# Setup order and the lead of the row maxima at the start of a two-layer AdaLN transformer kernel

## What is computed

```
mod = (silu(L0_c) @ L0_wmod).reshape(8, 6, 1, 128)
sa, ca, ga, sb, cb, gb = mod[:, 0], ..., mod[:, 5]
h = layernorm(x) * (1 + ca) + sa
q, k, v = h @ Wq + bq, h @ Wk + bk, h @ Wv + bv          # per head
scores = where(causal, -1e9, q @ k.T / sqrt(8))
x = x + ga * ((softmax(scores) @ v) @ Wo + bo)
```

## Time and profile before

| | |
|---|---|
| median of 3 runs | 1028.89 us (1027.29 to 1029.31) |
| the profiled execution | 1028.94 us, its span 1027.2 us |
| PE busy | 931.0 us (91%) |
| DVE busy | 776.5 us (76%) |
| ACT busy | 747.8 us (73%) |
| POOL busy | 541.3 us (53%) |
| chain that ended last | reaches back only into the last stage |

### The profile page before, as it was taken

One profiled execution on the slowest core, in us unless ns is written; L12 is line 12 of the kernel. 1 busy time (PEld: TensorE's weight loads), 2 busy tenths in 40 slices (PEclk: granted clock), 3 DMA queues, 4 the chain that ended last, 5 costly groups with the idle time before them and its releaser, 6 DMA issues. The chain is left out here.

```text
span 1027.2 us, 23002 instructions
## 1 busy us (share of the span) xinstructions
PE 931.0 (91%) x8664; PEld 513.0 (50%) x8664; DVE 776.5 (76%) x1319; ACT 747.8 (73%) x1380; POOL 541.3 (53%) x755
## 2 busy tenths in 40 slices
PE   4789989889888999999999799999999999989896
PEld 3234343343436888888888533333333333333575
DVE  4778878878864776767777678979788898994476
ACT  2388878878786566666665488888888888889663
POOL 4376766677632121322111078687777869666343
PEclk8599999999999999999999999999999999999999
DMA  7323332221104522425233021211202021100011
GB/s 181 96 74 121 114 104 78 74 76 50 51 26 124 167 82 74 114 90 148 61 106 96 20 84 30 59 35 53 75 14 77 13 84 35 56 13 14 25 32 52
DMA packets 63598, 73.91 MB, mean 72 GB/s; under 512 B 14136, under 2 KB 46008, under 8 KB 63104
## 3 DMA queue, kind: packets, MB, share of 16 engines
q1 hardware_dynamic: 62336, 69.23, 23.5%
q10 hardware_dynamic: 1152, 3.21, 1.0%
HBM read 39.24 MB, written 2.77 MB: 41 GB/s over the span
## 5 line engine op out<-in xcount | busy, mean ns | idle before, releaser
L872 ACT ACTIVATE at_E<-at_Sb 128x512 f32<-128x512 f32 x832 | 440.9, 597 | 75.7 <-PE at_Sb L718 70.2
L944 DVE TENSOR_REDUCE mx<-at_Mb 128x2 f32<-128x1024 f32 x242 | 280.6, 1216 | 40.3 <-PE at_Mb L681 39.1
L718 PE MATMUL at_Sb<-QP,KP 64*128 64x512 bf16 (+3 forms) x1024 | 202.3, 342 | 16.7 <-ACT full_k L419 7.1
L766 PE MATMUL at_Ob<-at_E,VP 128*32 128x256 f32 (+2 forms) x2816 | 204.5, 371 | 2.2 <-POOL at_E L1046 1.0
L1046 POOL TENSOR_TENSOR at_E<-at_E,factor 128x512 f32<-128x512 f32 x128 | 162.3, 1273 | 65.3 <-ACT at_E L872 55.7
L681 PE MATMUL at_Mb<-KP,QP 62*128 62x512 bf16 x996 | 169.7, 348 | 8.5 <-DVE mx L944 6.5
L947 DVE TENSOR_REDUCE mx<-at_Mb 128x2 f32<-128x768 f32 (+1 forms) x128 | 136.7, 1085 | 52.9 <-PE at_Mb L681 51.8
L1057 POOL TENSOR_SCALAR_AFFINE_SELECT at_E<-at_E 128x512 f32<-128x512 f32 x128 | 80.0, 645 | 71.8 <-ACT at_E L872 71.8
L718 PEld LDWEIGHTS at_Sb<-QP,KP 64*128 64x128 bf16 x1024 | 73.5, 95 | 82.6 <-ACT at_E L872 37.9
L766 PEld LDWEIGHTS at_Ob<-at_E,VP 128*32 128x32 f32 x2816 | 58.2, 108 | 88.1 <-issue 65.6
L1498 DVE TENSOR_TENSOR ex_hh<-ex_R,ex_th 128x512 f32<-128x512 f32 x88 | 64.6, 734 | 49.4 <-ACT ex_th L1435 48.7
(11 more groups left out here) (213 smaller groups left out, 1441.8 us busy)
## 6 DMA issues: line engine op xcount, KB each, us to landing
QP<-q SPq DMA_DIRECT2D x96, 128.0 KB, 2.4
KP<-k SPq DMA_DIRECT2D x91, 128.0 KB, 2.4
ex_R<-rw_dram SPq DMA_DIRECT2D x32, 256.0 KB, 3.5
ctxN<-Oev SPq DMA_DIRECT2D x16, 256.0 KB, 2.5
denB<-rdram SPq DMA_DIRECT2D x64, 64.0 KB
ex_R<-rw_dram SPq DMA_DIRECT2D x16, 224.0 KB, 3.5
ex_R<-rw_dram SPq DMA_DIRECT2D x16, 192.0 KB, 3.3
ex_R<-rw_dram SPq DMA_DIRECT2D x16, 160.0 KB, 2.8
```

The costliest lines, as they stand in the source:

```text
L718: return pe.matmul(out[:, at:at + SEQ - q0], KP[p0:p0 + ROWS_H, b % 2, 2 * g + a, kt * P:(kt + 1) * P], QP[p0:p0 + ROWS_H, b % 2, 2 * g + ...
L766: last = pe.matmul(Ob[VW * i:VW * (i + 1), 0, q0:q1], weights_of(b, G, kt, i, q0), moving, start=(kt == 0 and q0 == 0), stop=False, skip_g ...
L872: nc.scalar.activation(dst, src, ACT.Exp).then_inc(s["s_read"], 1)
L944: v.tensor_reduce(mx[:, G % 2, :, t % 2, t // 2], src, AX.X, ALU.max).then_inc(s["m_read"], 1)
```

## The change

In the setup: x of batch 0 is loaded ahead of c; POOL's zero fill of VP moves ahead of `front_powers`; batch 0's `front_normalise` moves from POOL to DVE; on PE the transposes of `xn` move ahead of bv times Wo.

In layer 0's attention: nine beats of maxima instead of eleven stand ahead of beat 0 (ten maxima ahead of the first score), and beats 2 and 5 hold two maxima each, the second at the end of PE's beat, so that the lead is eleven again from there. `max_T(1)` moves from beat 2 to beat 4, `max_T(0)` to beat -2. `shifts(G)` follows the table `shifts_at` (one beat after the last maximum of the group): beat -3 for group 0, 3 for group 1, as before from group 2 on. Statistics and `xn` of batch 1 move to beats -2 and -1.

```diff
         @block.sync
-            sp.dma_start(cT[:], dram["c"]).then_inc(s["c"], 16)
             sp.dma_start(x[:, 0:SEQ].rearrange("p (t d) -> p t d", t=TILES),
                          dram["x"][0].rearrange("(t p) d -> p t d", p=P)).then_inc(s["x0"], 16)
+            sp.dma_start(cT[:], dram["c"]).then_inc(s["c"], 16)
...
             g.memset(sb["ones"][:], 1.0)
+            g.memset(sb["VP"][:], 0.0).then_inc(s["zero"], 1)
             front_powers(g, sb, front, 0)
-            front_normalise(g, sb, front, 0)
-            g.memset(sb["VP"][:], 0.0).then_inc(s["zero"], 1)
...
+            t.wait_ge(s["ident"], 1)
+            front_transpose(t, sb, front, 0, fb[:, 0, :])
             t.wait_ge(s["columns"], 16)
...
-            t.wait_ge(s["ident"], 1)
-            front_transpose(t, sb, front, 0, fb[:, 0, :])
...
             front_aggregate(v, sb, front, 0)
+            front_normalise(v, sb, front, 0)
...
-        LEAD = 11 if causal else LEAD1
-        START = -LEAD if causal else 0
+        START = -9 if causal else 0
+        DOUBLE_AT = (2, 5) if causal else ()
...
+        first_max = 2 if causal else 0
...
-            if (beat + 4) % BPG == 0 and 0 <= (beat + 4) // BPG < ALLG:
+            if (beat + 4) % BPG == 0 and first_max <= (beat + 4) // BPG < ALLG:
                 out.append(("max", (beat + 4) // BPG))
+            if causal and beat in (-2, 4):
+                out.append(("max", 0 if beat < 0 else 1))
...
-        def m_of(beat):
-
-            m = beat + LEAD
-            return divmod(m, BPG) if 0 <= m < BPG * ALLG else None
+        def ms_of(beat):
+
+            m = beat + (9 if causal else LEAD1) + sum(at < beat for at in DOUBLE_AT)
+            return [divmod(i, BPG) for i in range(m, m + 1 + (beat in DOUBLE_AT)) if 0 <= i < BPG * ALLG]
...
+            for m in ms_of(beat):
+                m_slot[("max",) + m] = len(m_slot)
+                if m[1] == BPG - 1:
+                    shifts_at[beat + 1] = m[0]
...
-                if m_of(beat) is not None:
-                    max_score(*m_of(beat))
+                for m in ms_of(beat)[0:1]:
+                    max_score(*m)
...
+                for m in ms_of(beat)[1:]:
+                    max_score(*m)
...
-                if causal and beat == -4:
+                if causal and beat == -2:
                     v.wait_ge(sb["x1"], 16)
...
-                G, off = divmod(beat + LEAD - BPG, BPG)
-                if off == 0 and 0 <= G < ALLG:
-                    shifts(G)
-                if causal and beat == -3:
+                if beat in shifts_at:
+                    shifts(shifts_at[beat])
+                if causal and beat == -1:
                     front_powers(p, sb, s, 1)
                     normalise(1)
```

More of the change, by code:

```diff
@@ L607, in out_of @@
             return n - 1 if at == OUT_AT and 1 <= n <= last_b else None
-        def m_of(beat):
-            m = beat + LEAD
-            return divmod(m, BPG) if 0 <= m < BPG * ALLG else None
-        s_slot, m_slot = {}, {}
+        def ms_of(beat):
+            m = beat + (9 if causal else LEAD1) + sum(at < beat for at in DOUBLE_AT)
+            return [divmod(i, BPG) for i in range(m, m + 1 + (beat in DOUBLE_AT)) if 0 <= i < BPG * ALLG]
+        s_slot, m_slot, shifts_at = {}, {}, {}
         for name in (("ln", 0), ("q", 0), ("k", 0), ("v", 0)):
@@ L618, in attention_phase @@
             s_slot[("max", 0)] = len(s_slot)
-            for m in range(LEAD):
+            for m in range(LEAD1):
                 m_slot[("max",) + divmod(m, BPG)] = m
@@ L623, in attention_phase @@
                 s_slot[name] = len(s_slot)
-            if m_of(beat) is not None:
-                m_slot[("max",) + m_of(beat)] = len(m_slot)
+            for m in ms_of(beat):
+                m_slot[("max",) + m] = len(m_slot)
+                if m[1] == BPG - 1:
+                    shifts_at[beat + 1] = m[0]
             if out_of(beat) is not None:
@@ L962, in _ @@
             for beat in range(START, END):
-                if m_of(beat) is not None:
-                    reduce_max(*m_of(beat))
+                for m in ms_of(beat):
+                    reduce_max(*m)
                 if out_of(beat) is not None:
```

## The result

The changed kernel took 1035.11 us in the median of its first 4 runs (1032.15 to 1036.4), against 1028.09 for the kernel before beside it (4 runs): ratio 1.0065, 95% interval 1.0038 to 1.0092. Ten more runs of the same kernel gave a median of 1033.34 against 1029.53 (33 runs), ratio 1.0043 (1.0021 to 1.0066), that is +4.4 us (+2.2 to +6.8). It is slower. The forecast of +3.5 us (a ratio of 1.0034) lies in the second interval, and just under the lower end of the first; the first median, 1035.11, is only 0.09 us inside the upper end of the forecast range (1035.2). The profiled execution took 1032.15 us, with a span of 1030.4 against 1027.2.

A forecast was written before the change was run, and what follows sets the result against it. The prediction saw PE busy 91% of the span, and waits setting the first group's pace. Setup -0.7, stall +2.6 and clock +1.6 gave +3.5 us on 1028.94: 1032.4 us, range 1029.7 to 1035.2.

The forecast's parts named there:

- buy two exps, no more: First group: the first scores run some 2.5 us earlier, but batch 1's transposes still wait for xn, so only two exps are gained.
- The stall's size: Beat 4: PE waits for group 1's shifts behind q's split, +3.4 us, less 0.8 won back: +2.6, bounds 1.9 to 3.4.
- the setup's -0.7: Setup: projections start at about 11.4 in place of 12.14, -0.7 us, bounds 0 to -1.0.
- the stall without the clock: Rival: PE's clock rises as early as before and stays, leaving setup and stall: +1.9 us, 1030.9 us; chance 0.18.
- The clock's size: First group: PE's clock rises later or falls again around beats 5 and 6: +1.6 us, between 0 and 2.6.
- Every later group by the same amount: After the first group: the first Oev is 2 to 5 us later, and each later group is equally late.
- the stall is taken up: Rival: PE waits in beat 4, but slack in later groups wins nearly all back: 1028.2 to 1029.5 us; chance 0.09.
- no stall: Rival: POOL finishes split and shifts before PE reaches the transpose in beat 4: -0.7 to -2.3, about 1026.8 us; chance 0.05.
- The clock costs more: Rival: the clock falls in the stall and again, or more stretches run at half clock: +5 to +7, about 1034.8 us; chance 0.10.
- the main case: Stall in beat 4 and slower clock behind it together: 1031.6 to 1034.2 us, chance 0.58.
- nothing: Setup: loading x ahead of c delays c by at most one queue place, at no cost to PE.
- the consequence I drew from it: Setup: the moved fill holds the second silu step until 5.2, so xn ends at about 9.4 and the sum is 0.2 us higher.

The follow-up runs named there:

- shift_first: The changed kernel with group 1's shifts one beat earlier on POOL, ahead of the split of batch 1's q: 1028.71 us, ratio 0.9996 to the kernel before.
- fill_stall: The changed kernel with ten matmuls of unread result on PE directly ahead of its wait for group 1's shifts: 1030.79 us, ratio 1.0011 to the kernel before.
- after_again: The whole changed kernel measured once more, with no edit: median 1033.34 us in ten runs, ratio 1.0043 to the kernel before.
- stats_old_lead: The changed kernel's setup with the old lead of eleven maxima and batch 1's statistics, rstd and xn ahead of the first loop: 1027.43 us, ratio 0.9991.
- fill_late: The changed kernel with POOL's zero fill of VP behind front_powers again, beside xn on DVE: 1035.2 us, ratio 1.0068 to the kernel before.
- late_shift: The kernel before with only group 1's shifts put behind q's split on POOL and their transpose moved to beat 4: 1032.14 us, ratio 1.0039.

## Why the prediction was right, and where it was off

**Direction and mechanism: right.** Every sign that the prediction named for the stall is there: first scores at 34.18 (forecast 34.8), then a wait of 2.77 us (over 2), `nm` and `nmx` right behind the split, 2.97 us of waiting at L667 (2 or more), a clock back at 0.50, the first `Oev` 2.4 us later (2 to 5). That the earlier first scores "buy two exps, no more" agrees with the runs: q's projection starts 1.76 us earlier (41.05 against 42.81), of which 1.45 came with the first maximum, and with the stall gone (shift_first) the earlier scores and the setup together are worth -0.4 us (-1.9 to +1.0).

**The stall's size.** Forecast +3.4 gross. In the profiled executions the next maximum starts 1.74 us later (48.23 against 46.49) although the first maximum was 1.45 us earlier: 3.2. Net of what comes back the forecast was +2.6. With the setup's -0.7 this is the +1.9 of the rival "the stall without the clock"; fill_stall is that case made real, at +1.9 by its median and +1.1 by its ratio. Its first `Oev` stands 2.6 us behind that of shift_first (57.66 against 55.03), and its median, each against the kernel before beside it, 2.7 us above; by the ratios it is 1.5 us. So the term was about right, or too large.

**The clock's size.** Forecast +1.6 within 0 to 2.6. Measured by fill_stall: 2.6 us by the medians of the two kernels, which were not measured side by side (1033.34 less 1030.79), 3.3 by the ratios, and 1.1 to 1.9 us by the traces up to the first `Oev`. By the totals the term was too low, by the traces it was right; which holds is open. If the ratios are right in both terms, the forecast total is partly luck, as 1.1 us too much in the stall stood against 1.7 us too little in the clock. The upper end of its range, that the 3.33 busy us between 50 and 55 fill the stretch, is what came: PE has 5.00 of 5 us there in the changed kernel.

**How it was carried on.** "Every later group by the same amount" held to within 0.4 us in the trace of the changed kernel, +2.4 to +2.2 at layer 0's last `Oev`. That depends on the pair of traces. after_again is 3.5 us late at the first `Oev` and still at the 20th of 32, and 2.0 us late from the 21st on. The rows of these two, the 20th and the 21st, are in the kernel before:

```profile
216.98 0.58 ACT L900 ACTIVATE Oev<-at_Ob 128x512 f32<-128x512 f32 x1
227.72 0.58 ACT L900 ACTIVATE Oev<-at_Ob 128x512 f32<-128x512 f32 x1
```

and in after_again, with its busy time in a stretch of the earlier trace rows:

```profile
220.51 0.57 ACT L907 ACTIVATE Oev<-at_Ob 128x512 f32<-128x512 f32 x1
229.69 0.57 ACT L907 ACTIVATE Oev<-at_Ob 128x512 f32<-128x512 f32 x1
```

```profile
221.00:224.00 3.00, 1.43 (x19) 0.56 (x16) 3.00 (x3) 2.00 (x5) 2.92 (x2) 1.00 0.15 46
```

This step takes 10.7 us in the three traces whose clock is at 0.50 in it (before, after, stats_old_lead) and 9.2 us in the nine whose clock stays at 1.00. So the lateness was handed on nearly in full, as forecast, and a fall of the clock that comes in some executions, with and without the change, moves the total by 1.5 us. One pair of traces therefore can't give the cost at the span's end, where the changed kernel is at +3.2; what arose behind layer 0's attention was not followed up. The rival "the stall is taken up" falls by this, as "no stall" did with the 2.97 us at L667. "The clock costs more" (about 1034.8 us) is not so clearly out: the median of the first four runs, 1035.11, lies there, nearer than to the forecast of 1032.4. The ten later runs, with a median of 1033.34, lie in the span of the main case (1031.6 to 1034.2), and only single ones of them above it.

**Setup: the term was small, and one trace misled.** What did not hold is the start of PE's chain, which the prediction left where it was, x ahead of c costing "nothing". c itself came later (ACT's tanh at 3.82 against 2.66), which put DVE's statistics behind it from 4.02 to 4.36; PE's wait for wmod covered that. PE's first matmuls wait for wmod, which stands third in both orders, and yet they start at 6.55 to 7.59 (mean 7.09) in the eight traces that have the new setup whole, and at 6.41, 6.44 and 6.88 in the three with the old one. The moved fill is not the reason, since they start at 7.23 in fill_late too; the order of the two loads was not tried by itself. So the loads are the likely reason, not a shown one, and the two groups overlap (6.55 against 6.88). The 0.5 us between the means takes back about half of what PE gains by having bv times Wo (1.06 us) behind the transposes. The rest of the chain follows as forecast, only later: the projections begin at 11.42 to 12.46, mean 11.96, against a mean of 12.30 (12.14, 12.16, 12.60): 0.3 us, not 0.7. The 1.45 us at the first maximum is mostly not the change: late_shift has the old setup, and its first maximum stands at 24.00. The difference between that trace and the one of the kernel before is in the four projection matmuls: they took 1.96 us there and 3.78 in the trace that the prediction read the earlier trace rows, with the same code ahead of them.

**The fill and the second silu step.** In the trace of the changed kernel L241 (L243 before) took 0.90 us instead of some 0.2, up to 5.18, where the fill ended at 5.14. The rule of the Trainium skill ("SBUF — State Buffer", section "Who interferes with whom"), that a DVE instruction in a two-port mode and one of GpSimd exclude each other, agrees with that, and with the 4.09 us of `xn` in fill_late; which mode an instruction was in, no trace shows. But the consequence I drew from it, statistics at 5.4 and `xn` at about 9.4, did not come: the statistics are recorded from 4.36 on, beside the held instruction, and `xn` was ready at 8.17.

**The size of the first result.** +7.0 us in the first 4 runs and +3.8 in the next 10, by medians, are one kernel. The ten later executions run from 1028.99 us at a mean granted clock of 0.982 to 1036.63 at 0.975, the time by and large falling as the clock rises. In the profiled one of these ten the busy time by stretch reads:

```profile
45.00:50.00 5.00, 2.05 (x20) 0.78 (x16) 2.53 (x3) 1.60 (x4) 4.11 (x8) 0.62 0.00 0
```

The clock was 0.62 here and 0.92 in the other trace of the same code, and the first `Oev` came at 59.41 instead of 58.37. So the length of the half clock around the stall varies by execution, as does the fall near 222 us told above. Whether these two alone make the spread is not shown, since executions without a profile leave no trace.

## What to carry to other kernels

When a schedule is shifted by a few steps, list for each in-order queue what each moved instruction now stands behind: here three instructions of 0.2 us behind a split of 3 us cost 0.3 to 0.4%, more than the shorter lead and the new setup had won together (0.4 us, not told from nothing). Before shortening what stands ahead of the first useful work, see what the second needs: the first scores came 3.8 us earlier and PE then waited 2.8 us for a normalisation that could have been computed while DVE and POOL waited for a DMA. Price the clock beside the stall: behind this stall of 3 us it cost 1.1 to 1.9 us by the traces and 2.6 by the medians. And compare more than one trace of each kernel before reading a difference of 1 to 2 us at a late point.

## What was unexpected in the hardware

- The four setup projections (128x512 float32) took 3.78 us in one trace and 3.75 in another (fill_late), and 1.95 to 2.54 in the ten others, while the granted clock is recorded as 1.00 from 12 to 16 us in the traces of before, of the changed kernel, of late_shift and of fill_late alike. 3.78 us is near twice 1.95 us, as 2.07 us is near twice the 1.12 us of a pair in the first group; why it is so in these two traces is open. The record of the granted clock does not tell them apart; the matmul's own duration does.
- A DVE instruction held by POOL's fill (L241, 4.28 to 5.18) did not hold back the next four on the same engine (L357, from 4.36), as the trace records them; the other seven traces with this setup show the same.
- Ten matmuls without use, 2.33 us of PE work, ahead of a wait made the kernel faster than the same kernel with PE standing still, by 2.6 us in the medians (the intervals of the two ratios overlap by 0.04%).
